# A selective-scan kernel: ten-column scans, and the last states carried through GpSimd

## The reference, cut to what matters

```python
xn   = x * rsqrt(mean(x * x) + 1e-6) * norm_w
xb, gate = split(xn @ W_in.T)
xc   = silu(conv4(xb) + conv_b)
dt   = soft_clamp(softplus(xc @ W_dt.T + b_dt), 0.001, 0.1, 0.5)
Bp, Cp = xc @ W_B.T, xc @ W_C.T
dA   = exp(soft_clamp(dt * A, -8, 8, 0.5))           # per step, d, n
# one step t of the recurrence:
h    = h * dA_t + dt_t * B_t * xc_t
if t % 10 == 0: h = h * min(20 / norm(h), 1)         # norm over all d and n of a sequence
y_t  = sum_n(h * C_t) + D * xc_t
out  = layernorm(2 * x + scale * ((y * silu(gate)) @ W_out.T))
```

## Time and profile before

| what | us |
| --- | --- |
| median of three runs | 2820.96 |
| profiled execution | 2822.23 |
| its span, first to last instruction | 2820.4 |
| DVE busy in the span | 2401.1 (85%) |
| PE busy | 2604.8 (92%) |
| ACT busy | 2247.3 (80%) |
| POOL busy | 2137.4 (76%) |

### The profile page before, as it was taken

The page is one execution under the profiler, slowest core; times in us unless marked ns, Lnnn a source line. Parts: engine busy times, 40 slices in busy tenths (PEclk is TensorE's granted clock), DMA queues, the critical chain, the costliest instruction groups (busy, mean ns, idle before and its releaser), DMA issues. The chain is left out here.

```text
span 2820.4 us, 51549 instructions
## 1 busy us (share of the span) xinstructions
PE 2604.8 (92%) x16812; PEld 2393.3 (85%) x16812; DVE 2401.1 (85%) x3373; ACT 2247.3 (80%) x5011; POOL 2137.4 (76%) x2236
## 2 busy tenths in 40 slices
PE   5799999999999999999999999999999974899992
PEld 4799999999999999999999999999999873677762
DVE  1899999999999999999999999999999995221224
ACT  5999999999999999999999999999999941111113
POOL 0688888888888888888888888888888872434324
PEclk9999999999999999999999999999999996999996
DMA  1222222222222222332322222322222222134226
GB/s 60 64 70 83 75 79 80 76 79 81 73 78 75 79 81 75 79 81 72 81 75 75 83 73 80 81 75 77 80 70 81 71 67 92 38 101 97 64 49 249
DMA packets 153972, 225.72 MB, mean 80 GB/s; under 512 B 46056, under 2 KB 92776, under 8 KB 152552
## 3 DMA queue, kind: packets, MB, share of 16 engines
q1 hardware_dynamic: 131208, 188.98, 23.4%
q0 software_dynamic: 9216, 12.59, 2.6%
q10 hardware_dynamic: 13280, 20.86, 2.2%
HBM read 189.26 MB, written 33.05 MB: 79 GB/s over the span
## 5 line engine op out<-in xcount | busy, mean ns | idle before, releaser
L638 POOL TENSOR_TENSOR H<-H,CB 128x640 f32<-128x640 f32 x832 | 1222.6, 1483 | 207.2 <-DVE H L476 207.1
L476 DVE TENSOR_TENSOR_SCAN H<-DA,PM 128x704 f32<-128x704 f32 x832 | 1316.9, 1603 | 2.2 <-ACT DA L278 2.0
L391 ACT ACTIVATE DA<-DT,SM 128x160 f32<-128x160 f32 x3328 | 1116.1, 424 | 1.5 <-POOL DT L606 0.3
L660 PE MATMUL YB<-H,ID 128*128 128x160 f32 x6656 | 1046.9, 309 | 0.5 <-POOL H L638 0.5
L660 PEld LDWEIGHTS YB<-H,ID 128*128 128x128 f32 x6656 | 985.2, 191 | 16.7 <-issue 11.2
L451 DVE TENSOR_TENSOR PM<-PM,BB 128x640 f32<-128x640 f32 x832 | 677.0, 814 | 1.5 <-DMA BB<-Bd 1.5
L278 ACT ACTIVATE DA<-DA 128x2560 f32<-128x2560 f32 x208 | 485.4, 2334 | 1.7
L666 PE MATMUL PAZ<-XN,WIN 128*128 128x160 f32 x1664 | 254.9, 307 | 3.0 <-DVE VV L536 1.8
L676 PEld LDWEIGHTS PAZ<-XB,CD 128*128 128x128 f32 x1664 | 237.5, 188 | 16.8
L617 POOL TENSOR_TENSOR FC<-SN,HALF 128x4 f32<-128x4 f32 x206 | 233.2, 1132 | 21.7 <-DVE SN L482 7.8
L685 PE MATMUL PAZ<-XC,WDT 128*128 128x160 f32 x1664 | 243.0, 299 | 3.9 <-DVE XC L509 3.9
(11 more groups left out here) (152 smaller groups left out, 2793.5 us busy)
## 6 DMA issues: line engine op xcount, KB each, us to landing
BB<-Bd SPq DMA_DIRECT2D x208, 320.0 KB, 3.5
CB<-Cd SPq DMA_DIRECT2D x208, 320.0 KB, 3.4
W<-in_w ACTq DMA_DIRECT2D x16, 1024.0 KB
XT<-in_xT SPq DMA_DIRECT2D x52, 160.0 KB, 2.2
XR<-in_xp SPq DMA_DIRECT2D x416, 20.0 KB
X2d<-VV SPq DMA_DIRECT2D x416, 20.0 KB
YA<-VV SPq DMA_DIRECT2D x416, 20.0 KB
HI<-YA SPq DMA_DIRECT2D x6, 1024.0 KB, 9.9
```

Of the source, the lines that this page charges most:

```text
L391: eng.activation(DA[:, c0:c0 + 2, :, a, m, 1:11].rearrange("p c b t -> p b c t"), DT[:, j % 2, a].rearrange("p b (c t) -> p b c t", c=2), ...
L476: eng.tensor_tensor_scan(H[:, q % 3, u], a0, DBX(u), 0.0, ALU.mult, ALU.add).then_inc(s_scan, 1)
L638: eng.tensor_tensor(h, h, cb, ALU.mult).then_inc(s_hc, 1)
L660: mm = eng.matmul(yv, ID[:], hv[:, :, :, n, 0:10], start=False, stop=n == 15)
```

## The change

Scans become ten columns long, 640 instead of 704. The carried state no longer has a column of its own. The state after the ten steps of q - 2 is multiplied by the first decay of q on POOL (EG), the first decay is then set to 0 in DA (a memset), and DVE adds EG times the factor FC to the first column of the product with B (carry, now one scalar_tensor_tensor per u instead of one copy per two). Because y's rows are now the scan's own steps, the halos, the rotating CS, and NM are gone; the clamp's factor goes into the last column of CB on POOL instead. POOL's multiply with C, PE's y_sum, z_out and the transfer of C come later: POOL lags the scans by six u, y_sum works on q - 2 and q - 3, H has four buffers instead of three. Some blocks move within the turn: on ACT the first Exp of the next chunk ahead of the Ln at step 13, the gate's Tanh from step 14 to 15, and a new DUE; on POOL the layer norm to two turns after its chunk, step 2, and DT and XN behind that step's multiply; on SP the results' transfers to step 4; on PE the output projection from step 10 to 11.

```diff
-        DA = sb("DA", [128, 4, 8, 4, 16, 11])
-        H = sb("H", [128, 3, 4, CH])
+        DA = sb("DA", [128, 4, 8, 4, 16, 10])
+        H = sb("H", [128, 4, 4, CH])
...
-            DUE = [0, 3, 3, 10, 12, 18, 19, 27, 35, 41, 43, 50, 56, 56, 58, 64, 64]
+            DUE = [0, 3, 3, 11, 14, 20, 22, 30, 38, 44, 46, 54, 61, 64, 64, 64, 64]
...
-                        eng.activation(CS[32:48, q0:q0 + 2, :, 1:10], pv[32:48, :, :, 0:9],
-                                       ACT.Copy).then_inc(s_bcs, 1)
-                        eng.activation(CS[32:48, q0 + 1, :, 0:1], pv[32:48, 0, :, 9:10],
-                                       ACT.Copy).then_inc(s_bcs, 1)
...
-                        eng.activation(CS[32:48, (q0 + 2) % 4, :, 0:1], pv[32:48, 1, :, 9:10],
-                                       ACT.Copy).then_inc(s_bcs, 1)
+                        eng.activation(CS[32:48], pv[32:48], ACT.Copy).then_inc(s_bcs, 1)
...
-                    if s == 12:
+                    if s == 13 and ok(i + 1):
+                        eng.wait_ge(s_z64, 64 * (i + 2))
+                        exp_a(i + 1, 0)
+                    if s == 13:
...
-                    if s == 14 and ok(i + 1):
+                    if s == 15 and ok(i + 1):
                         j = i + 1
                         eng.wait_ge(s_gt, 2 * (j + 1))
...
-                    if s == 15 and ok(i + 1):
-                        eng.wait_ge(s_z64, 64 * (i + 2))
-                        exp_a(i + 1, 0)
...
             def carry(q, u):
...
                 if q < 2:
-                    eng.memset(o, 0.0).then_inc(s_ca, 1)
+                    return
+                o = DBX(u).rearrange("p (a t) -> p a t", t=10)[:, :, 0]
+                if u == 0:
+                    eng.wait_ge(s_fac, q - 1)
+                    eng.wait_ge(s_ea, q - 1)
+                eng.wait_ge(s_m1, 4 * q + u + 1)
+                eng.scalar_tensor_tensor(o, EG[:, u], FC[:, q % 2, u:u + 1], o, ALU.mult, ALU.add).then_inc(s_ca, 1)
...
-                    eng.tensor_copy(o, CAR[:, u:u + 2].rearrange("p u a -> p (u a)")).then_inc(s_ca, 1)
...
                     if live and u % 2 == 0:
                         mult(q, u)
-                        carry(q, u)
                         mult(q, u + 1)
...
+                    if live and u % 2 == 0:
+                        carry(q, u)
+                        carry(q, u + 1)
                     if live:
                         scan(q, u)
-                    if u == 0 and 0 <= q - 3 < NQ:
+                    if u == 2 and 0 <= q - 3 < NQ:
                         z_out(q - 3)
...
+                    if u == 2 and 0 <= q + 1 < NQ:
+
+                        p = q + 1
+                        a0 = DA[:, (p // 2) % 4, 4 * (p % 2):4 * (p % 2) + 4].rearrange("p b a n t -> p b (a n) t")[:, :, :, 0]
+                        eng.wait_ge(s_da, p + 1)
+                        if p >= 2:
+                            if p >= 3:
+                                eng.wait_ge(s_ca, 4 * (p - 2))
+                            eng.wait_ge(s_scan, 4 * (p - 1))
+                            eng.tensor_tensor(EG[:], H[:, (p - 2) % 4].rearrange("p u (a t) -> p u a t", t=10)[:, :, :, 9], a0,
+                                              ALU.mult).then_inc(s_ea, 1)
+                            eng.wait_ge(s_ea, p - 1)
+                        eng.memset(a0, 0.0).then_inc(s_a0, 1)
+                    if u == 2 and 0 <= q - 1 < NQ:
+
+                        p = q - 1
+                        eng.wait_ge(s_cb[p % 2], one(p))
+                        if p < NQ - 2:
+                            cl = CB[:, p % 2, :, :, 9]
+                            eng.wait_ge(s_fac, p + 1)
+                            eng.tensor_tensor(cl, cl, FC[:, p % 2].unsqueeze(1).to_broadcast([128, 16, 4]),
+                                              ALU.mult).then_inc(s_cbs, 1)
+                            eng.wait_ge(s_cbs, p + 1)
+
+                    p, v = (q - 2, u + 2) if u < 2 else (q - 1, u - 2)
+                    if 0 <= p < NQ:
+                        h = H[:, p % 4, v].rearrange("p (a n t) -> p a n t", a=4, n=16)
+                        cb = CB[:, p % 2, :, v, :].unsqueeze(1).to_broadcast([128, 4, 16, 10])
+                        eng.wait_ge(s_scan, 4 * p + v + 1)
+                        eng.tensor_tensor(h, h, cb, ALU.mult).then_inc(s_hc, 1)
                     if s == 14 and ok(i + 2):
                         j = i + 2
                         eng.wait_ge(s_dth, j + 1)
...
-                        eng.tensor_tensor(CAR[:], H[:, p % 3].rearrange("p u (a t) -> p u a t", t=11)[:, :, :, 10],
-                                          FC[:, p % 2].unsqueeze(2).to_broadcast([128, 4, 64]),
-                                          ALU.mult).then_inc(s_car, 1)
...
+                    if s == 2 and ok(i - 2):
...
                     if u == 0:
-                        y_sum(q - 2, 11, 16)
+                        y_sum(q - 3, 11, 16)
...
                     if u == 2:
-                        y_sum(q - 1, 0, 6)
+                        y_sum(q - 2, 0, 6)
                     if u == 3:
-                        y_sum(q - 1, 6, 11)
+                        y_sum(q - 2, 6, 11)
```

More of the change, by code:

```diff
@@ L19 @@
 NQ = 2 * NC
-CH = 704
+CH = 640
 def ok(j):
@@ L79, in ssm_phase @@
         FC = sb("FC", [128, 2, 4])
-        CAR = sb("CAR", [128, 4, 64])
+        EG = sb("EG", [128, 4, 64])
         PM = ctx.enter_context(nc.psum_tensor("PM", [128, 2048], F32))
@@ L99, in ssm_phase @@
             sem("bcs"), sem("sp"), sem("dth"), sem("tg"), sem("z64"), sem("da"), sem("x2t"), sem("hsq"))
-        s_halo, s_sgh, s_dx, s_dxh, s_hc = sem("halo"), sem("sgh"), sem("dx"), sem("dxh"), sem("hc")
-        s_min, s_dt, s_xn, s_pow, s_fac, s_car = (
-            sem("min"), sem("dt"), sem("xn"), sem("pow"), sem("fac"), sem("car"))
+        s_halo, s_dx, s_cbs, s_hc = sem("halo"), sem("dx"), sem("cbs"), sem("hc")
+        s_min, s_dt, s_xn, s_pow, s_fac, s_ea, s_a0 = (
+            sem("min"), sem("dt"), sem("xn"), sem("pow"), sem("fac"), sem("ea"), sem("a0"))
         s_ve, s_sd, s_x2 = sem("ve"), sem("sd"), sem("x2")
@@ L113, in ssm_phase @@
         KD = 0.5 / (0.0495 + 1e-8)
-        PRE_C, PRE_CV, PRE_W, N_PRE = 9, 27, 29, 34
+        PRE_C, PRE_CV, PRE_W, N_PRE = 7, 25, 27, 30
         loads = [
@@ L134, in NP @@
         def NP(q):
-            return YB[1 - q % 2][:, 256:384]
+            return YB[q % 2][:, 256:384]
         def two(j):
@@ L175, in parts @@
         def parts(j):
-            lo, hi = max(T * j - 10, 0), min(T * j + 10, L)
+            lo, hi = max(T * j - 9, 0), min(T * j + 11, L)
             cut = min(hi, (lo // 128 + 1) * 128)
-            return [(l, h, l - (T * j - 10)) for l, h in ((lo, cut), (cut, hi)) if h > l]
+            return [(l, h, l - (T * j - 9)) for l, h in ((lo, cut), (cut, hi)) if h > l]
         def lg_done(j):
@@ L214, in sync_program @@
                                       ).then_inc(s_bb[p % 2], 16)
-                    if u == 1 and 0 <= q + 1 < NQ:
-                        p = q + 1
+                    if u == 3 and 0 <= q < NQ:
+                        p = q
                         c, g = p // 2, p % 2
@@ L225, in sync_program @@
                         lg_out(eng, i - 3)
-                    if s == 2 and ok(i - 2):
+                    if s == 4 and ok(i - 2):
                         j = i - 2
@@ L287, in scalar_program @@
                             eng.wait_ge(s_nrm, q - 1)
-                        eng.activation(SQ[:], H[:, (q - 1) % 3].rearrange(
-                            "p u (a t) -> p u a t", t=11)[:, :, :, 10], ACT.Square).then_inc(s_hsq, 1)
+                        eng.activation(SQ[:], H[:, (q - 1) % 4].rearrange(
+                            "p u (a t) -> p u a t", t=10)[:, :, :, 9], ACT.Square).then_inc(s_hsq, 1)
                     if s == 0 and ok(i + 3):
@@ L569, in gpsimd_program @@
                     q = 4 * i + r
-                    if s == 5 and ok(i + 1):
+                    if s == 9 and ok(i + 1):
                         j = i + 1
@@ L583, in gpsimd_program @@
                         eng.tensor_copy(XB[:, :, :, 0:3], XB[:, :, :, 20:23]).then_inc(s_halo, 1)
-                    if s == 14 and ok(i - 1):
-                        j = i - 1
-                        eng.wait_ge(s_mv, 2 * (j + 1))
-                        eng.tensor_scalar(NM[:], MVR[:, :, 0], -1.0, 0.0, ALU.mult, ALU.add).then_inc(s_ve, 1)
-                        eng.tensor_scalar(SD[:], MVR[:, :, 1], 1.0, 1e-5, ALU.mult, ALU.add).then_inc(s_ve, 1)
-                        eng.wait_ge(s_ve, 2 * (j + 1))
-                        eng.tensor_tensor(SD[:], SD[:], HALF[0:80, 0:2], ALU.pow).then_inc(s_sd, 1)
-                        eng.wait_ge(s_sd, j + 1)
-                        for g in range(2):
-                            eng.tensor_scalar(VV[:, g], VV[:, g], NM[:, g:g + 1], SD[:, g:g + 1],
```

(32 more changed lines are left out.)

87 lines of the change are left out of this document (28 added, 59 removed).

## The result

The changed kernel takes 3050.3 us (median of 4 runs, 3049.99 to 3051.67), the kernel before beside it 2820.6: a ratio of 1.0815, 95% interval 1.0797 to 1.0834. The direction was forecast, the size was not: 2873 with a range to 2930.

A forecast was written before the change was run, and what follows sets the result against it. The kernel before was taken as bound by a ring ACT, PE, ACT (43.2 us a turn), DVE beside it at 43.15. The turn goes from 43.26 to 44.2: +47, tail +7, last turns -2, so 2873 us, range 2812 to 2930.

The forecast's parts named there:

- Ring E: Norm_sum, POOL's blocks and lagging multiplies, PE's y sum and norm, DVE to norm_sum: longest ring, 44.2 us a turn.
- ACT's ring alone: Rival: the ring ACT, PE, ACT sets the pace; turn 43.1 to 43.4, 2815 to 2834 us; chance 22%.
- DVE sets the pace: Rival: DVE is the bound and its saving of 1.66 us a turn arrives, 2743 us; chance 10%.
- The signs named: Turn near 44.2; DVE idle before norm_sum or XC; PE waiting for H; POOL over 93% busy, not waiting for scans.
- POOL's leg: POOL from norm_sum's start through blocks, layer norm and lagging multiplies to the last multiply's end: 22.1 us.
- The two blocks: POOL's work in the middle of each q, with EG, memset and CB's product: from 2.25 to 3.17 us each.
- PE's leg: PE from the y sum's first matmul through the queued projections to the norm's end: 11.0 us.
- DVE's leg: DVE from the norm_sum that waits for PE's norm to the next N, norm_sum's start: 11.0 us.
- POOL dearer: Rival: EG at 1.51, CB's product at 0.8; turn 46.2, 2974 us (range 2905 to 2974); chance 12%.
- The rule on strides: GpSimd reading SBUF with steps over 8 bytes costs half again per element: EG 1.13, turn 44.8, some 2903 us.
- DVE's own work: Shorter scans, eight copies fewer, sixteen carries more on DVE: from 43.15 to 41.5 us a turn (41.2 to 42.6).
- ring B: Norm_sum, POOL's XN, PE's line 666, ACT, XC on DVE, next norm_sum: 43.8 us a turn.

The follow-up runs named there:

- e5: Changed kernel with one word of POOL's layer norm changed, the mean added instead of subtracted (output not the reference's): 2920.8 us.
- e1: Changed kernel with the layer norm as before the change, the mean negated into NM and added on POOL instead of subtracted: 2931.5 us.
- e3: Changed kernel with eight extra 128-column matmuls on PE before the y sum of a chunk's last q: 2989.3 us.
- e6: e1 with EG's second input replaced by a constant, so only one input is strided (output not the reference's): 2896.2 us.
- e12: Changed kernel with the edits of e1 and e8, layer norm later (ahead of step 6's factor), its stores at SP's step 9, XC behind two multiplies: 2866.2 us.
- e4: Kernel before the change with each DVE carry copying 8 of its 128 columns: 2818.0 us against 2823.2, one run each.
- e8: Kernel before the change with three decay tanh moved from ACT's step 2 into step 1: 2817.4 us against 2821.4, ratio 0.9988.
- e7: Kernel before the change with the edits of e4 and e8 together: 2797.0 us.

## Why the prediction was right in direction and wrong in size

**The ring was the right one.** Ring E holds each of the ten turns from 1020 to 1500, joint by joint, and the rivals "ACT's ring alone" and "DVE sets the pace" are out: DVE waits and POOL waits for norm_sum. The signs named came: PE waits for H, POOL does not wait for scans, DVE waits before norm_sum and XC. POOL's busy share is 90% in nine turns, not over 93%, since the ring is longer than POOL's work.

**The step that failed is the size of ring E's terms.** Forecast 44.2; measured, in the turn shown, 48.14, and 47.73 on the mean.
- POOL's leg, 22.1, was 24.27. The layer norm ("twice 0.551 for VV", 2.26 in all) takes 3.52, from 1466.82 to 1470.34: +1.26. Its edit read as "NM is gone", a saving; that the remaining instruction now subtracts, where the earlier trace rows had timed one that adds, was not priced. e5 shows that this word is the whole of it. The two blocks, 3.17 each, take 3.46 and 3.77: +0.89. Of this EG has 0.73 (1.12, not 0.754). The memset (0.56 long, a step of 0.42, not 0.35) and CB's product (0.41 with its wait, not 0.44) nearly cancel.
- PE's leg, 11.0, took 10.89 at the upper clock and 12.56 behind the long wait. The prediction let PE wait for H, and took the time behind the wait from rows without one. The wait of 2.28 us has itself been lengthened by the subtraction: without that it is 1.14 and the clock stays (e1). e3 prices the slower clock: 61 us.
- DVE's leg, 11.0, is 11.28: the carries.

In time: of the 177 us between 2873 and 3050, 129 hang on the subtraction (e5: 68 on POOL, 61 by way of the clock), 35 on EG (e6, measured on e1), and if the two add up, 13 are left for the rest. e6, which has both edits and NM's instruction besides, is at 2896.

**POOL dearer** was the rival of the right kind, but with the wrong carrier: at 2.0 a turn it put 2974, from EG at 1.51 and CB's product at 0.8. The range was drawn from new operations alone; an old one that the diff edits had no bounds.

**The rule on strides.** EG takes 1.12 with two strided inputs and 0.75 with one, 1.49 times (e1, e6). The Trainium skill, "GPSIMD Engine Reference", section "Performance pitfalls for Q7 kernels", puts a step over 8 bytes at about half as much again per element. EG agrees in size with the estimate of 1.13 that the prediction drew from it. But CAR's one strided input has such a step too, at 0.754 for 256 columns, and XN's packed ones are at 0.867 for 320, 2.9 against 2.7 ns a column: here the surcharge came with the second strided input, not with the first, so part of the agreement is luck. The prediction had the better price beside its sum and left it out.

**DVE's own work** was to fall from 43.15 to 41.5. It is 43.5 in the changed kernel and 42.8 in e12, where dt_x (DVE's product of dt and xc) takes 0.49. The scan came as forecast (1.469 for 1.467). The carry did not: 0.277 long, not 0.21; two in 0.47, so 0.19 a step, inside the bounds (0.10 to 0.20) at their far end: 16 times 0.06 is +1.0. And dt_x (line 425) takes 0.892 where it had 0.511: +0.8 for two a turn. In e1 the same line takes 0.50 beside POOL's factor and 0.96 beside its multiply of two inputs:

```profile
1366.08 0.50 DVE L426 TENSOR_TENSOR PM<-DT,XC 128x320 f32<-128x320 f32 x1
...
1398.32 0.96 DVE L426 TENSOR_TENSOR PM<-DT,XC 128x320 f32<-128x320 f32 x1
```

```profile
1366.21 1.26 POOL L581 TENSOR_TENSOR FC<-SN,HALF 128x4 f32<-128x4 f32 x1 [0.73 <-DVE SN L470]
...
1394.67 4.26 POOL L613 TENSOR_TENSOR H<-H,CB 128x640 f32<-128x640 f32 x3
```

The dear one lies beside POOL's multiply for its first 0.61 us and ends 0.35 after that multiply. The lag put DVE's one product of two SBUF inputs beside POOL's multiplies. That DVE's products with two SBUF inputs contend with GpSimd is what the Trainium skill says ("GPSIMD Engine Reference", section "Key points"); this trace agrees, and the size, 0.96 against 0.50, is its own. It did not set the pace here.

**What bounded the kernel before** was read rightly: e4 and e8 gain 5 and 4 us, e4's within the spread of single runs, and e7 gains 23. A saving on DVE alone was worth 0.1 us a turn at most.

**Slips in the prediction's sums.** None moves the forecast. The rule on strides adds 1.13 in place of EG's 0.84, which holds a wait of 0.083; like for like its turn is 44.95, and some 2911. DVE's lower bound by its own terms is 41.0, not 41.2, ring B's sum 43.87, and the lower end for ACT's ring 2819, not 2815.

## What to carry over

When a change closes a ring through several engines, price every instruction on it again, those that the diff edits by one word as well as the new ones: a ring has no slack, so each 0.1 us here is paid in every turn. Take the time behind a new wait on PE at both clock levels: here the lower one came behind eight of ten waits of 2.2 to 2.3 us, and behind none of the ten of 1.5 us earlier in the same turns. Where two limits stand side by side, relieving one shows nothing; test them together before an edit that relieves one and lengthens a third.

## What the runs showed of the hardware

- A GpSimd tensor_scalar of 80x256 that subtracts and then multiplies takes 1.225 us, one that adds and multiplies 0.554, with the same operands (after, e5).
- A GpSimd product of 256 columns takes 0.751 us with one strided input, the other a constant, and 1.12 with two (e6, e1).
- Adding matmuls in front of a wait made the kernel 61 us faster, since the granted clock stayed at 1.00 (e3). PE idle for 2.20 to 2.29 us was followed by 0.50 in eight turns of ten; a wait of 2.22 stands on both sides, so its length alone does not decide (after).
- DVE's product of two SBUF inputs, 320 columns, takes 0.50, or 0.96 when its first 0.61 lie beside a GpSimd multiply of two SBUF inputs (e1).
- A DVE scan costs 0.133 us less for 64 columns less (1.602 to 1.469), 2.1 ns a column; an instruction of 64 columns with PSUM in and out still takes 0.277.
